# Expert outputs written in block order by ScalarE's DMA queue and gathered per token tile, sixteen blocks led by the first eight tiles

## The chip, the cores and the metric

The kernel runs on one core of one Trainium2 chip. The metric is the device time of one execution in microseconds (us), the median of several. The engines are TensorE (PE in the profile, its weight loads PEld), VectorE (DVE), ScalarE (ACT), GpSimd (POOL) and SyncE (SP, which here only issues DMAs). Each has its own instruction stream; a q behind an engine's name (ACTq) marks what its sequencer does itself: register instructions, loads of a word from SBUF into a register, branches and the issuing of DMAs.

## What is computed

Input x has 4 sequences of 512 tokens with 256 values, 2048 tokens in all. The reference, cut to what matters:

```python
x = x + attn(layernorm(x))       # linear recurrence with complex gates, two projections
xn = layernorm(x)
w, idx = gate(xn, gate_w)        # 6 of 32 experts per token, out of 4 of 8 groups
y = einsum('tei,te,edi->td', silu(xn @ w11) * (xn @ w33), c, w22)   # c: weights of the chosen experts
x = x + y + silu(xn @ sw1.T) * (xn @ sw3.T) @ sw2.T                 # shared expert
```

All values are float32. Each expert has a hidden width of 128.

## The kernel before

**Head.** The tokens are cut into 16 tiles of 128 and into 6 chunks (`CHUNKS`: 2, 2, 4, 4, 2, 2 tiles). A list of stages, written out by hand for each engine, takes the chunks through norm, recurrence, output projection, second norm, router (`logits`, `scores`, `choose`) and `places`, which works out for each token and each of its 6 experts a row in a DRAM tensor `bucket_rows`. There each expert has a bucket of its own. GpSimd sends the rows there with one indirect DMA for each tile and choice (L427, 96 in all). A row holds 256 values and, for each of 32 experts, a pair: weight and number of the row of `choice_rows` where the expert's output for this token must go.

**Table.** VectorE then works out a table of 127 blocks of 128 rows (L927 to L955): first row in `bucket_rows`, expert, column of the expert's pair. TensorE turns it into rows (L1191 to L1193), and it ends as integers in `tabs`. Around this TensorE does the shared expert (`shared_gate_up`, L1165, eight groups of 8 matmuls of 512 columns, and `shared_down`, L1178, four groups of 16 of 256 columns), with ScalarE (`shared_silu`, L612) and VectorE (`shared_hidden`, L960, `shared_out`, L964) behind it.

**Block loop.** SyncE loads the 128 rows of a block (L359) eight blocks ahead, once all rows are scattered and `tabs` is there. TensorE's step s transposes block s (L1220), makes gate and up of block s-1 (L1228, 8 matmuls) and the down projection of block s-2 (L1235). ScalarE's step s reads the expert of block s from `tabs` (L623), copies its gate and up weights (L625), copies the transposed rows (L630, waits for L1220) and applies silu to block s-1 (L617, waits for L1228). VectorE's step s multiplies silu and up of block s-1 (L985), scales the output of block s-2 (L992) and copies the pair of block s (L980). GpSimd scatters each block's output to `choice_rows` (L441, 127 indirect DMAs). Two buffers stand behind most of these steps, eight behind the outputs. Steps 16 to 63 run in hardware loops of 16 steps on the engines, the others are written out.

**Sum.** `choice_rows` has the six outputs of a token one behind another. From step 70 on SyncE loads them by tile (L367, 768 KB each), and VectorE adds them to `resid` one by one (L1016), at most two per step. ScalarE issues twelve stores (L646). The last tiles come after the last block; TensorE sums one of them (L1261).

## Time and profile before

| | us |
|---|---|
| median of 3 runs (lowest, highest) | 449.61 (448.42, 450.6) |
| the profiled execution | 450.83 |
| its span | 449.1 |

| part of the span | from | to |
|---|---|---|
| head, to the first transposes of a block | 0 | 228.4 |
| block loop, to the last scaled output | 228.4 | 432.2 |
| rest: last scatters, loads, sums, stores | 432.2 | 449.1 |

The profile has the busy time of each engine, the span in 40 slices, the chain of work that ended last, groups of instructions, and a timeline with start and length of each instruction. In the timeline a bracket holds the idle time of the engine ahead of an instruction and what ended it; "issue" is idle time with nothing in the profile that was waited for. What a sequencer does itself stands under the engine's name with a q, and does not count as busy.

### The profile page before, as it was taken

What the parts mean: (1) busy time and instruction counts of PE and PEld (TensorE: products, weight loads), DVE (VectorE), ACT (ScalarE), POOL (GpSimd) and SP (SyncE); (2) the same over time, 40 slices, a digit from 0 to 9 for tenths busy, and PEclk for the clock granted to TensorE, in tenths of its full rate; (3) what the DMA queues carried; (4) which work ended last, traced back from release to release, by engine and by line L of the source; (5) the groups of instructions that cost most, each with busy time, mean ns of one, the idle gap of its engine ahead of it and who ended that gap; (6) DMA issues with size and microseconds to landing.
All of it is one profiled execution on the core that took longest, in us unless ns stands there. A gap on an engine that the chain in (4) does not pass through costs nothing.

```text
span 449.1 us, 9145 instructions
## 1 busy us (share of the span) xinstructions
PE 376.1 (84%) x2120; PEld 301.2 (67%) x2121; DVE 294.3 (66%) x990; ACT 260.7 (58%) x585; POOL 231.6 (52%) x242
## 2 busy tenths in 40 slices
PE   2777696965976778399889999999999998998935
PEld 2644263745645563155579999999999997997924
DVE  3669688999988824612235555555567777777982
ACT  2678978768575132011157777767777776776710
POOL 2000000752778777777516666666656665663750
PEclk9898867595785687689999999999999999999996
DMA  8990000220335999333347666666689889879724
GB/s 241 405 339 2 0 0 1 74 102 15 118 118 201 413 430 380 130 128 128 117 145 215 188 195 182 204 188 191 191 265 354 255 248 300 303 208 336 244 83 174
DMA packets 41850, 87.70 MB, mean 195 GB/s; under 512 B 7204, under 2 KB 32295, under 8 KB 41296
## 3 DMA queue, kind: packets, MB, share of 16 engines
q1 hardware_dynamic: 28384, 54.77, 36.7%
q0 software_dynamic: 10704, 30.07, 18.6%
q10 hardware_dynamic: 2720, 2.40, 1.7%
q8 instruction: 15, 0.25, 0.3%
q14 instruction: 27, 0.22, 0.2%
HBM read 49.81 MB, written 39.71 MB: 199 GB/s over the span
## 4 chain that ended last, share of the span: by engine, by line
PE 50%; DVE 19%; ACT 9%; DMA 8%; issue 8%; POOL 3%; DVEq 1%; SPq 1%; ACTq 0%; POOLq 0%
PE PS L1228 17%; PE PS L1235 8%; PE PS L1165 7%; DMA payload_and_xn_t<-choice_rows 5%; PE PS L1220 4%; PE PS L1121 3%; POOL choice_rows L441 3%; PE PS L1178 3%; DMA resid<-in_x 2%; PE PS L1076 2%; ACT L605 1%; DVE st L682 1%; PE PS L1261 1%; ACT payload_and_xn_t L555 1%; DMA choice_rows<-block_out_s,block_meta 1%
## 5 line engine op out<-in xcount | busy, mean ns | idle before, releaser
L441 POOL DMA_INDIRECT choice_rows<-block_out_s,block_meta x127 | 127.0, 1000 | 86.0 <-issue 58.3
L427 POOL DMA_INDIRECT bucket_rows<-payload_and_xn_t,dest x96 | 101.9, 1062 | 116.2 <-DVE dest L874 88.2
L1228 PE MATMUL PS<-block_rows_t,block_gate_up_weights 128*128 128x128 f32 x1016 | 134.9, 276 | 0.0
L1228 PEld LDWEIGHTS PS<-block_rows_t,block_gate_up_weights 128*128 128x128 f32 x1016 | 123.4, 192 | 1.1 <-ACT block_rows_t L630 0.9
L625 ACT ACTIVATE block_gate_up_weights<-expert_weights 128x512 f32 x127 | 80.0, 630 | 35.6 <-issue 29.6
L1235 PE MATMUL PS<-expert_weights,block_hidden_t 128*128 x254 | 76.3, 382 | 3.8 <-DVE block_hidden_t L985 3.8
L992 DVE TENSOR_SCALAR block_out_s<-PS,block_meta 128x256 f32<-128x256 f32 x127 | 61.2, 482 | 0.0
L985 DVE TENSOR_TENSOR block_hidden_t<-block_silu_t,PS 128x128 f32<-128x128 f32 x127 | 36.3, 286 | 24.2 <-ACT block_silu_t L617 22.0
L630 ACT ACTIVATE block_rows_t<-PS 128x256 f32<-128x256 f32 x127 | 46.5, 366 | 7.6 <-PE PS L1220 7.6
L1220 PE MATMUL PS<-ident,block_rows_s 128*128 128x128 f32 x254 | 48.6, 273 | 1.4 <-DVE resid L964 1.3
L980 DVE COPY block_meta<-block_rows_s 128x2 f32 x127 | 22.0, 173 | 41.7 <-issue 41.4
L617 ACT ACTIVATE block_silu_t<-PS 128x128 f32<-128x128 f32 x127 | 35.0, 276 | 18.7 <-PE PS L1228 18.0
L1220 PEld LDWEIGHTS PS<-ident,block_rows_s 128*128 128x128 f32 x254 | 35.6, 141 | 14.5 <-DVE resid L964 1.7
L1016 DVE TENSOR_TENSOR resid<-resid,payload_and_xn_t 128x256 f32<-128x256 f32 x90 | 37.8, 421 | 10.1 <-DMA payload_and_xn_t<-choice_rows 9.2
L1235 PEld LDWEIGHTS PS<-expert_weights,block_hidden_t 128*128 128x128 f32 x254 | 38.5, 192 | 4.9 <-issue 4.9
L1165 PE MATMUL PS<-payload_and_xn_t,sw_s 128*128 128x512 f32 x64 | 33.3, 676 | 1.2 <-DVE turn_abs L960 1.2
L1121 PE MATMUL PS<-w_in_and_w_out,block_rows_s 128*128 128x256 f32 x96 | 25.8, 418 | 0.4 <-DVE block_rows_s L797 0.4
L1165 PEld LDWEIGHTS PS<-payload_and_xn_t,sw_s 128*128 128x128 f32 x64 | 13.8, 219 | 17.8 <-issue 16.0
L1076 PE MATMUL PS<-expert_weights,gate_blockdiag 128*128 128x256 f32 (+1 forms) x48 | 22.6, 634 | 1.7 <-ACT expert_weights L499 1.5
L1121 PEld LDWEIGHTS PS<-w_in_and_w_out,block_rows_s 128*128 128x128 f32 x96 | 20.3, 213 | 4.6 <-issue 0.7
L605 ACT ACT_TABLE_LOAD x18 | 23.1, 1283 | 0.3
L1087 PE MATMUL PS<-ident,payload_and_xn_t 128*128 128x128 f32 x32 | 7.4, 392 | 15.9 <-ACT payload_and_xn_t L555 12.0
(185 smaller groups left out, 459.1 us busy)
## 6 DMA issues: line engine op xcount, KB each, us to landing
block_rows_s<-bucket_rows SPq DMA_DIRECT2D x127, 160.0 KB
payload_and_xn_t<-choice_rows SPq DMA_DIRECT2D x16, 768.0 KB, 6.5
bucket_rows<-pad_rows SPq DMA_DIRECT2D x1, 5120.0 KB, 26.3
expert_weights<-in_experts SPq DMA_DIRECT2D x1, 4224.0 KB, 14.0
expert_weights<-in_experts SPq DMA_DIRECT2D x1, 3456.0 KB, 16.3
expert_weights<-in_experts SPq DMA_DIRECT2D x1, 2688.0 KB, 18.3
resid<-in_x SPq DMA_DIRECT2D x4, 512.0 KB, 9.3
choice_rows<-block_out_s,block_meta POOLq DMA_INDIRECT x127, 3.2
```

Source lines behind the costliest of these rows:

```text
L427: nc.gpsimd.indirect_dma_start(out=bucket_ap[:, :], out_offset=bass.IndirectOffsetOnAxis(ap=dest[:, t, k:k + 1], axis=0), in_=PAY[:, t, :] ...
L441: nc.gpsimd.indirect_dma_start(out=choice_ap[0:rows, :], out_offset=bass.IndirectOffsetOnAxis(ap=meta_id[:, slot, 1:2], axis=0), in_=yy[:, ...
L625: A(ws[:, r, :], W[:, bass.ds(first, KD * 2 * P)], ACT.Copy)
L630: A(xT[:, r, :], PS[:, r, 0:D], ACT.Copy).then_inc(s_xt, 1)
L985: TT(hh[:, r, :], sg[:, r, :], PS[:, 2 + r, P:2 * P], M).then_inc(s_hh, 1)
L992: TSC(yy[:, slot, :], PS[:, 6 + r, 0:D], meta[:, weight, 0:1], None, M).then_inc(s_y, 1)
L1016: ins = TT(resid[:, n, :], resid[:, n, :], RINGS[:, n % RING, k, :], AD)
L1121: ins = mm(PS[:, 6 + t // 2, (t % 2) * D:(t % 2 + 1) * D], PROD[h][:, t * P:(t + 1) * P], wt, start=False, stop=(n == len(parts) - 1 and t ...
L1165: ins = mm(PS[:, bank, :], sw13_s[:, k, g, h * P:(h + 1) * P], XN2T[:, b, k, :], start=(k == 0), stop=(k == KD - 1))
L1220: ins = nc.tensor.transpose(PS[:, r, k * P:(k + 1) * P], xs[:, slot, k * P:(k + 1) * P], ident[:])
L1228: ins = mm(PS[:, 2 + r, g * P:(g + 1) * P], ws[:, r, (2 * k + g) * P:(2 * k + g + 1) * P], xT[:, r, k * P:(k + 1) * P], start=(k == 0), st ...
L1235: mm(PS[:, 6 + r, 0:D], hh[:, r, :], W[:, bass.ds(w + KD * 2 * P, D)], start=True, stop=True).then_inc(s_yp, 1)
```

## The change

- **Rows** hold 256 values and 32 weights: `ROW` is 288, not 320. `choose` and the padding lose the row numbers, two VectorE instructions per chunk.
- **Outputs** go to a DRAM tensor `bucket_outputs` in which each block's 128 rows follow one another. ScalarE's queue issues one plain DMA of 128 KB per block (`write_block`), four steps after the block's first step; its row is a fourth column of `tabs`, loaded for four blocks at once. The tensor is first filled with zeros by five DMAs of SyncE's queue during the head (16.6 MB in all, `s_clear`).
- **Gathers**: GpSimd no longer scatters outputs. For each token tile it gathers six times 128 rows of `bucket_outputs` into a ring of four tiles (96 indirect DMAs of 128 KB), as soon as enough blocks are written (`blocks_through`) and the ring's place is free. VectorE makes one add per step from step 59 on (`add_choice`), 70 up to step 128, and 26 after it. SyncE issues all stores. TensorE's sum of a tile is gone.
- **Leading blocks**: the first sixteen blocks of the table are whole blocks of the first eight tiles (`early_blocks`, some twenty small VectorE instructions ahead of `choose(4)`), so their loads wait for three chunks' scatters and not for six. The table has nine phases (288 entries per quantity, before 160) and four quantities (before three).
- **Order before the loop**: on TensorE `positions(4)`, `positions(5)` stand behind the first `shared_gate_up`, and a third one stands ahead of the table's matmuls. On VectorE the first two `shared_hidden` stand ahead of the table and inside it, and `output_rows` and `output_sources` come between the later ones.
- **Loops**: bodies of 8 steps over steps 8 to 119 on TensorE and ScalarE.

```diff
-    ROW = D + 2 * E
+    ROW = D + E
-    LP = 16
+    LP = 8
-    UNROLL_AT = 64
-    RING = 6
+    LOOPED = BLOCKS // LP * LP
+    RING = 4
+    EARLY_BLOCKS = 16
+    EARLY_TILES = 8
+    FIRST_ADD = 59
+    WRITE_LAG = 4
...
+            for n in range(NCH - 1):
+                part = slice(n * BLOCKS // (NCH - 1), (n + 1) * BLOCKS // (NCH - 1))
+                sp.wait_ge(s_gp, n + 1)
+                sp.dma_start(outputs_ap[part.start * P:part.stop * P].rearrange("(j p) d -> p j d", p=P),
+                             PADT[:, 0:D].unsqueeze(1).to_broadcast([P, part.stop - part.start, D])).then_inc(s_clear, 16)
...
-                nc.gpsimd.indirect_dma_start(
-                    out=choice_ap[0:rows, :], out_offset=bass.IndirectOffsetOnAxis(ap=meta_id[:, slot, 1:2], axis=0),
-                    in_=yy[:, slot % NY, :], in_offset=None,
-                    bounds_check=last_row, oob_is_err=False).then_inc(s_ys[slot % NY], 16)
+            def gather_outputs(n):
+
+                all_written(pool, blocks_through(phase_of(n)))
+                pool.wait_ge(s_src, n // TS + 1)
+                if n < RING:
+                    pool.wait_ge(s_resid, B)
+                for k in range(TOPK):
+                    if n >= RING:
+                        pool.wait_ge(s_added, added(n - RING, k))
+                    nc.gpsimd.indirect_dma_start(
+                        out=RINGS[:, n % RING, k, :], out_offset=None, in_=outputs_ap[0:BLOCKS * P, :],
+                        in_offset=bass.IndirectOffsetOnAxis(ap=source[:, n, k:k + 1], axis=0)).then_inc(s_cin[n % RING][k], 16)
...
+            first_outputs = [act.alloc_register(f"first_output{q}") for q in range(4)]
+
+            def write_block(j, u):
+
+                if u % 4 == 0:
+                    act.reg_load(first_outputs, tabs[0:1, bass.ds(j + 3 * P, 4)])
+                act.wait_ge(s_y, j + 1)
+                row = act.snap(first_outputs[u % 4], min_val=0, max_val=2 * P * P - P)
+                act.dma_start(outputs_ap[bass.ds(row, P), :], yy[:, u % NY, :]).then_inc(s_ys[u % NY], 16)
...
-            def store(n):
-                act.wait_ge(s_fin, n + 1)
-                act.dma_start(out_d[n], resid[:, n, :]).then_inc(s_out_act, 16)
+                if not isinstance(s, int) or s >= WRITE_LAG:
+                    write_block(s - WRITE_LAG, (u - WRITE_LAG) % LP)
...
-            with act.Fori(LP, UNROLL_AT, LP) as i:
+            with act.Fori(LP, LOOPED, LP) as i:
...
+            c.add(TT(PICKS, quant[:], PER_V.unsqueeze(1).to_broadcast([P, 4, V5]), M))
+            c.wait()
+            c.add(V.tensor_reduce(tabf[:, 0:4], PICKS, X, AD))
...
+            for m in range(done, NT * TOPK):
+                add_choice(*divmod(m, TOPK))
```

The first place is ScalarE's loop body. Before, a step is these seven rows; L623 is the word of `tabs`, L617 silu:

```order
L617 ACTIVATE block_silu_t<-PS 128x128 [waits block_gate_up_psum]
L623 ISA
L623 TENSOR_LOAD tabs
L624 ISA
L625 ACTIVATE block_gate_up_weights<-expert_weights 128x512
L629 REGISTER_ALU
L630 ACTIVATE block_rows_t<-PS 128x256 [waits block_transposed_psum]
```

In the changed kernel the same stretch, silu to the copy of the weights, reads so in a step that also loads four rows of the table:

```order
L643 ACTIVATE block_rows_t<-PS 128x256 [waits block_transposed_psum]
L630 ACTIVATE block_silu_t<-PS 128x128 [waits block_gate_up_psum]
L650 ISA
L650 TENSOR_LOAD tabs
L651 REGISTER_ALU
L652 ISA [waits block_out]
L653 DMA bucket_outputs<-block_out_s 128x256
L636 ISA
L636 TENSOR_LOAD tabs
L637 ISA
L638 ACTIVATE block_gate_up_weights<-expert_weights 128x512
```

Between silu of one block and the weights of the next there now stand the register instructions and the DMA of the write, and in every fourth step a second load.

The second place is TensorE between the head's stages and the table. Before:

```order
L1165 MATMUL PS<-payload_and_xn_t,sw_s 128x512 [waits gates,shared_weights_loaded]
...
L1165 MATMUL PS<-payload_and_xn_t,sw_s 128x512 [waits ln2_transposed]
...
L1133 MATMUL PS<-member,tri 128x32 [waits bucket_rows_known,projected,membership]
...
L1191 MATMUL PS<-ident,tabf 1x128 [waits block_table_columns,bucket_rows_known]
L1192 MATMUL PS<-ident,tabf 1x128
L1193 MATMUL PS<-ident,tabf 1x128
L1165 MATMUL PS<-payload_and_xn_t,sw_s 128x512 [waits shared_hidden]
```

And now (L1275 is the old L1165, L1242 the old L1133, L1303 the table):

```order
L1275 MATMUL PS<-payload_and_xn_t,sw_s 128x512 [waits gates,shared_weights_loaded]
...
L1242 MATMUL PS<-member,tri 128x32 [waits bucket_rows_known,projected,membership]
...
L1275 MATMUL PS<-payload_and_xn_t,sw_s 128x512 [waits ln2_transposed]
...
L1275 MATMUL PS<-payload_and_xn_t,sw_s 128x512 [waits shared_hidden]
...
L1303 MATMUL PS<-ident,tabf 1x128 [waits block_table_columns,bucket_rows_known]
```

The positions moved ahead of the second group of shared matmuls, and a third group moved ahead of the table.

## Rows read from the trace of the kernel before

**Rows 1.** The page: granted clock (tenths) and data in 40 slices; one group.

```profile
PEclk9898867595785687689999999999999999999996
...
GB/s 241 405 339 2 0 0 1 74 102 15 118 118 201 413 430 380 130 128 128 117 145 215 188 195 182 204 188 191 191 265 354 255 248 300 303 208 336 244 83 174
...
L1016 DVE TENSOR_TENSOR resid<-resid,payload_and_xn_t 128x256 f32<-128x256 f32 x90 | 37.8, 421 | 10.1 <-DMA payload_and_xn_t<-choice_rows 9.2
```

**Rows 2.** Timeline in the hardware loop: start, us, engine, line, operation, [idle before].

```profile
290.71 0.97 PEld L1228 LDWEIGHTS PS<-block_rows_t,block_gate_up_weights 128*128 128x128 f32 x8
...
291.09 0.63 ACT L625 ACTIVATE block_gate_up_weights<-expert_weights 128x512 f32 x1 [0.45 <-issue]
...
291.62 0.36 ACT L630 ACTIVATE block_rows_t<-PS 128x256 f32<-128x256 f32 x1
...
291.91 0.28 ACT L617 ACTIVATE block_silu_t<-PS 128x128 f32<-128x128 f32 x1
...
292.63 0.63 ACT L625 ACTIVATE block_gate_up_weights<-expert_weights 128x512 f32 x1 [0.44 <-issue]
...
293.80 0.97 PEld L1228 LDWEIGHTS PS<-block_rows_t,block_gate_up_weights 128*128 128x128 f32 x8
```

**Rows 3.** Timeline of a written-out step in which ScalarE issues a store.

```profile
341.61 0.28 ACT L617 ACTIVATE block_silu_t<-PS 128x128 f32<-128x128 f32 x1 [0.24 <-PE PS L1228]
341.61 0.36 ACTq L646 DMA_DIRECT2D out<-resid  x1
...
341.95 0.97 PEld L1228 LDWEIGHTS PS<-block_rows_t,block_gate_up_weights 128*128 128x128 f32 x8
...
342.74 0.63 ACT L625 ACTIVATE block_gate_up_weights<-expert_weights 128x512 f32 x1 [0.86 <-issue]
...
343.69 0.97 PEld L1228 LDWEIGHTS PS<-block_rows_t,block_gate_up_weights 128*128 128x128 f32 x8 [0.17 <-ACT block_rows_t L630]
```

**Rows 4.** Sequencer work by line, ns min/median/max: L623 at 276-301 and 340-345, L359.

```profile
L623 ACTq TENSOR_LOAD <-tabs x16: 274/492/525, 276.9 to 299.7; - x16
...
L623 ACTq TENSOR_LOAD <-tabs x4: 275/284/613, 340.1 to 344.9; - x4
...
L359 SPq FUSED_REGOPS  x127: 42/42/48, 224.1 to 417.9; - x127
...
L359 SPq DMA_DIRECT2D block_rows_s<-bucket_rows x127: 337/338/445, 224.3 to 418.1; - x127
```

**Rows 5.** Timeline from the table to the first block.

```profile
177.75 0.20 PE L1135 MATMUL PS<-member,ones 128*128 128x32 bf16 x2
...
180.39 0.32 DVE L927 SCALAR_TENSOR_TENSOR block_rows_s<-bucket_next 128x160 int32<-128x160 f32 x1
...
184.28 0.65 DVE L948 TENSOR_REDUCE tabf<-block_rows_s 128x3 f32<-128x480 f32 x1
...
188.12 6.31 PE L1165 MATMUL PS<-payload_and_xn_t,sw_s 128*128 128x512 f32 x8 [1.23 <-DVE turn_abs L960]
...
197.72 7.03 PE L1165 MATMUL PS<-payload_and_xn_t,sw_s 128*128 128x512 f32 x16
...
220.72 0.96 POOL L427 DMA_INDIRECT bucket_rows<-payload_and_xn_t,dest  x1 [0.30 <-issue]
...
227.13 1.22 DVE L964 TENSOR_TENSOR resid<-resid,PS 128x1024 f32<-128x1024 f32 x1 [3.81 <-PE PS L1178]
...
228.40 0.95 PE L1220 MATMUL PS<-ident,block_rows_s 128*128 128x128 f32 x4 [1.31 <-DVE resid L964]
```

**Rows 6.** Busy time by stretch: length; PE, PEld, DVE, ACT, POOL; clock, DMA share, GB/s.

```profile
350.00:375.00 25.00, 23.51 (x182) 21.72 (x181) 17.77 (x61) 17.12 (x46) 14.64 (x15) 1.00 0.83 256
```

**Rows 7.** Timeline of the end: last scaled block output, last store issued.

```profile
431.70 0.48 DVE L992 TENSOR_SCALAR block_out_s<-PS,block_meta 128x256 f32<-128x256 f32 x1
...
446.93 0.34 ACTq L668 DMA_DIRECT2D out<-block_rows_s  x1
```

**Rows 8.** The chain that ended last: start, length, what.

```profile
433.77 2.07 DMA choice_rows<-block_out_s,block_meta
```

More of the change, by code:

```diff
@@ L349, in _, with rows_scattered, load_block @@
             sp.wait_ge(s_outp, NCH)
-            for i in range(NCH):
-                sp.wait_ge(s_scat[i], 16 * TOPK * CHUNKS[i][2])
-            def load_block(j, slot, taken):
+            def rows_scattered(first, end):
+                for i in range(first, end):
+                    sp.wait_ge(s_scat[i], 16 * TOPK * CHUNKS[i][2])
+            early_chunks = next(i + 1 for i in range(NCH) if CHUNKS[i][0] * TS + CHUNKS[i][1] + CHUNKS[i][2] == EARLY_TILES)
+            rows_scattered(0, early_chunks)
+            first_rows = [sp.alloc_register(f"first_row{q}") for q in range(4)]
+            def load_block(j, u, taken):
+                if u % 4 == 0:
+                    sp.reg_load(first_rows, tabs[0:1, bass.ds(j, 4)])
                 if taken is not None:
@@ new lines, in _ @@
+            for j in range(EARLY_BLOCKS):
+                load_block(j, j, j - NXS + 1 if j >= NXS else None)
+            rows_scattered(early_chunks, NCH)
+            with sp.Fori(EARLY_BLOCKS, FIRST_STORE, LP) as i:
+                for u in range(LP):
+                    load_block(i + u, u, i + (u - NXS + 1))
+            with sp.Fori(0, STORE_TURNS, 1) as turn:
+                for u in range(TURN_ADDS):
+                    j = turn * TURN_ADDS + (FIRST_STORE + u)
+                    load_block(j, u, j - (NXS - 1))
+                    if u % (2 * TOPK) < 2:
+                        store_tile(u // (2 * TOPK) * 2 + u % (2 * TOPK), turn)
@@ L962, in shared_out, with output_sources @@
+            def output_sources(g):
+                at_least(dve, s_src, g)
+                dve.wait_ge(s_added, 1)
+                for t in range(TS):
+                    c.add(V.max(dv[:, t, :], dpos[:, g * TS + t, :]))
+                c.wait()
+                TSC(source[:, g * TS:(g + 1) * TS, :], dv[:, :, 0:TOPK], -1.0, None, AD).then_inc(s_src, 1)
             def shared_out(b):
@@ L974, in _ @@
                     shared_hidden(b + 1, 1)
+                if b == 0:
+                    output_rows()
+                if b > 0 and b + 1 < B:
+                    output_sources(b - 1)
+            for g in range(B - 2, B):
+                output_sources(g)
             def take_meta(j, slot, loads):
                 dve.wait_ge(s_xs[slot % NXS], loads)
-                col = dve.value_load(tabs[0:1, bass.ds(j + 2 * P, 1)], min_val=D, max_val=D + 2 * (E - 1))
-                V.tensor_copy(meta[:, slot, :], xs[:, slot % NXS, bass.ds(col, 2)]).then_inc(s_meta, 1)
+                col = dve.value_load(tabs[0:1, bass.ds(j + 2 * P, 1)], min_val=D, max_val=D + E - 1)
+                V.tensor_copy(meta[:, slot, :], xs[:, slot % NXS, bass.ds(col, 1)]).then_inc(s_meta, 1)
             def hidden(j, r):
@@ L1024, in _ @@
+            for s in range(LP + 3):
                 step(s, s)
-            with dve.Fori(LP, UNROLL_AT, LP) as i:
+            with dve.Fori(LP + 3, FIRST_ADD, LP) as i:
                 for u in range(LP):
-                    step(i + u, u)
-            for s in range(UNROLL_AT, BLOCKS + 2):
-                step(s, s)
-                for n in range(NT):
-                    if n in ADD_AT and ADD_AT[n] <= s < ADD_AT[n] + TOPK // ADD_RATE[n]:
-                        for _ in range(ADD_RATE[n]):
-                            add_choice(*divmod(adds["done"], TOPK))
@@ L1034, in _ @@
-            while adds["done"] < PE_SUM * TOPK:
-                add_choice(*divmod(adds["done"], TOPK))
-            for k in range(TOPK):
-                add_choice(NT - 1, k)
+                    step(i + u, u + 3)
+            with dve.Fori(0, ADD_TURNS, 1) as turn:
+                for u in range(TURN_ADDS):
+                    step(turn * TURN_ADDS + (FIRST_ADD + u), FIRST_ADD + u)
+                    add_choice(*divmod(u, TOPK), turn)
+            done = ADD_TURNS * TURN_ADDS
+            for s in range(FIRST_ADD + done, BLOCKS + 2):
+                step(s, s)
+                add_choice(*divmod(done, TOPK))
+                done += 1
```

415 lines of the change are left out of this document (226 added, 189 removed).

## The prediction

> **What bounds the kernel now.** I read the page first. TensorE's granted clock is at the higher of its two levels (2.4 GHz) nearly from the middle of the span to the end, where the block loop lies [rows 1]. Next the timeline of the loop. The weight loads of block s (L1228) begin at 290.71 and those two blocks later at 293.80, so a step takes 1.545 us [rows 2], and 127 steps make 196 of the 203.8 us between the first transposes at 228.40 [rows 5] and the last scaled output, 431.70 + 0.48 = 432.18 [rows 7]. TensorE sets this pace, but ScalarE is not far behind: in one step it starts the copy of the weights at 291.09, the copy of the transposed rows at 291.62, silu at 291.91, and the next weights at 292.63 [rows 2], with no idle time but "issue", its own sequencer. Last I read both ends: what frees the first block at 228.4 [rows 5], and what comes behind 432.2 [rows 7, 8].
>
> **The writes on ScalarE's queue.** This is the largest term. ScalarE and TensorE hold each other in a circle two blocks long, since weights and transposed rows have two buffers. From the start of the weight loads of block k to silu of block k: 291.91 - 290.71 = 1.20. From silu to the next weights: call it X, here 292.63 - 291.91 = 0.72. From there to the end of the copy of the rows: 291.62 - 291.09 + 0.36 = 0.89 [rows 2], and some 0.06 until TensorE starts block k+2. The circle is 2.15 + X and has two steps of time, 3.09; TensorE waits when X is above 0.94. The trace has one case to test this on. At 341.61 ScalarE issues a store of 0.36 right behind silu; X becomes 342.74 - 341.61 = 1.13, and TensorE starts block k+2 at 343.69 where 341.95 + 1.545 = 343.50 was due, 0.19 late, as 1.13 - 0.94 says [rows 3].
>
> In the changed kernel every step has such a DMA between silu and weights. A DMA with a row from a register takes 0.338 on its sequencer, a register instruction around 0.04 [rows 4], and a write has two or three: 0.44 in all. To what does that add? X in a looped step was 0.72 with a word's load of about 0.5, and such a load takes from 0.27 to 0.51 in the loop [rows 4]. So X is 0.72 + 0.44 = 1.16 with slow loads and 1.16 - 0.22 = 0.94 with fast ones. I take 1.06, between them, because in the written-out part the loads are mostly fast (0.284 of 0.275 to 0.613) and in the loop mostly slow (0.492) [rows 4], and the changed kernel's SyncE loads only every fourth step, so there is less to collide with. Every fourth step has a second load, of four words, with an instruction of 0.05 ahead. The trace has no load of four words; by the loads of one it is 0.33 to 0.66, and I take 0.45, the middle. These loads always hit the same of the two interleaved circles (the body has 8 steps, an even number), and the slower one sets the pace. Over four steps it needs 2 x (2.15 + X) + 0.45 = 6.87, or 1.717 per step, 0.172 over 1.545. ScalarE's loop has 112 steps (8 to 119): **+19.3 us**. With X at 0.94 and 0.33 it is 6.51 / 4 = 1.627, +9.2. With X at 1.16, another 0.107 if the issue takes 0.445 as SyncE's longest does [rows 4], and 0.66, it is 7.49 / 4 = 1.873, +36.8. The twelve written-out steps with a write have X near 0.8 to 0.9 and exceed the circle only with the four-word load: +0.6. Below nothing this term can't go: TensorE's own work is the 1.545.
>
> What a page says on this stands apart from the sum. The Trainium skill, Perfetto Trace Analysis, section on the hardware DMA instruction, says that the reported time of such an instruction includes waiting for a lock on the descriptor generator that two sequencers share. SyncE's range of 0.337 to 0.445 agrees with it weakly [rows 4]; if every write waited for a whole issue of SyncE, X would grow by 0.34 and the loop by a further 19 us.
>
> **What leaves the loop.** Of 25 us from 350 to 375 TensorE idles 1.5 [rows 6], and the stretch from 400 to 426 reads alike. In these VectorE waits for tiles of 768 KB that arrive late, with TensorE behind it. The gathers come earlier: tiles 0 and 1 can be gathered from about step 52, twelve of them take GpSimd some 15 us at the 0.96 + 0.30 per indirect DMA of the scatters [rows 5], and the first add is at step 59. Each later pair is likewise some ten steps ahead. **-3.0 us**. VectorE's step has one add of 0.421 [rows 1] where it had up to two, but more waits on registers; it keeps some 0.2 to 0.3 of slack at 1.717 per step, and I cost it at nothing.
>
> **The head.** Before, two things ended almost together: the shared expert, with `shared_out` at 227.13 + 1.22, and the scatters, the last of them issued at 220.72 for 0.96 [rows 5], with the first load of a block 2.6 behind it, at 224.3 [rows 4]. The leading blocks take the second out. The first moves little. TensorE has 10.3 us between 177.8, when the first positions are being made behind the second group of shared matmuls, and the third group at 188.12 [rows 5], of which positions and table fill 1.8. It now puts the third group in there. But VectorE's table, 180.39 to 184.93 before [rows 5], grows: 288 entries for 160, and the product and the reduction over four quantities have 1152 elements where 480 took 0.65 [rows 5], so about 1.4 each. With the two longer scans, three more products and a shared product of 0.7 inside, the table takes some 11.5. Places come some 3 us sooner, so it begins at 178 and ends near 189.5; with 1.3 for the matmuls TensorE goes on at 191. What is left then (five groups of 3.5, as 7.03 for two shows, four `shared_down` of about the same, some 1.4 of waiting for the last silu and product, and 2.8 for one group at the lower clock, as 6.31 for 3.5 shows [rows 5]) is 35.7, and the end 226.7, against 227.1. Each `choose` lacks 0.5 of VectorE's work, some of it on the path: 1 us more. Together **-1.5 us**, from +2 to -8.5. The zeros cost nothing: five writes of 3.3 MB from 20 us on, and from the fourth slice to the eleventh (34 to 123 us) the page has 0 to 118 GB/s where others have 400 [rows 1]. `output_rows` and `output_sources` lie beside TensorE's shared matmuls.
>
> **The end.** From 432.18, where the last output is scaled, to 449.1 is 16.9 us before [rows 7]. Now GpSimd is late. Tiles 12 and 13 need 115 blocks; the last of these is written by ScalarE at step 118, ten steps ahead of the last scaled output (which I call 0), and lands some 2.1 later [rows 8]. So their twelve gathers begin at -13.4 and take 12 x 1.26 to 1.7. Tile 14 follows to 9.3 and tile 15 to 16.8. The last gather lands 2.2 on, at 18.7; the last add takes 0.43, and the store 449.1 - 446.93 = 2.2 [rows 7]: 21.4. VectorE's 26 adds (11 us) hide behind the gathers. **+4.5 us**, from 0 if a gather takes 1.0, to +8.
>
> **Sum.** -1.5 - 3.0 + 19.3 + 0.6 + 4.5 = +19.9. The span becomes 469.0, and with the 1.7 us around it 470.7, against the profiled 450.8, which is itself 1.2 above the median. I give 470.
>
> **Rivals.** *ScalarE hides the writes.* For it: a sequencer runs ahead of its engine when it needn't wait; and the Trainium skill, DMA: Bandwidth & Descriptors, section on issuing engines, calls the sequencer's time for starting a DMA usually small beside the DMA. Against it: the 0.19 at 343.69, after just one such issue [rows 3]. Then all is as above without 19.9 of the loop: 450.8.
>
> *The head gives more, and the writes are hidden too; faster.* The point is when the table ends: if VectorE has it by 184, TensorE has no gap at all in the shared expert, and 10.3 - 1.8 = 8.5 come off and not 1.5. 450.8 - 8.5 - 3.0 + 4.5 = 443.8. VectorE would have to do the larger table in 6 us, and X would have to stay under 0.94; against that stand the 0.65 for 480 elements and the 0.36 of an issue [rows 3, 5].
>
> *The loop is slower still.* VectorE with its waits on registers becomes the bound, or the writes wait for the lock, or TensorE's clock falls to its lower level in the new gaps. At 1.9 per step it is +40 in the loop: 492. The gaps of 0.2 in each step are short, and in 350 to 375 the clock stayed at 1.00 with 1.5 us of idle time [rows 6].
>
> **Numbers.** Forecast, loop bound by ScalarE, 455 to 489: 0.75. Writes hidden, about 451: 0.09. Faster: 0.07. Slower still: 0.09. From 451 to 489 holds about 0.8. A measurement can tell about 0.5% from no change. Faster by over 0.5% (under 447.4): 0.08; within: 0.07; slower: 0.85.
>
> **What would show it.** In the profile after, looped steps are 1.63 to 1.87 long, TensorE's weight loads of L1228's successor wait for ScalarE's copy of the transposed rows in most of them, and silu to weights is 0.94 to 1.3, with a DMA of 0.34 inside. Steps longer by 0.3 come every fourth. The first transposes come at 225 to 228, and behind the last scaled output lie some 21 us, with gathers back to back. Wrong I'd be if X stayed under 0.94, if the wait before those weight loads named VectorE or a block's load, or if gathers began late enough to hold up adds in the loop.

## The result: 476.1 us, slower by 5.8%

| | before | after |
|---|---|---|
| median, us (lowest, highest, of 4 runs each) | 450.11 (448.42, 450.67) | 476.09 (474.18, 477.0) |
| span of the profiled execution | 449.1 | 475.2 |
| head, to the first transposes | 228.4 | 226.8 |
| block loop, to the last scaled output | 203.8 | 221.8 |
| rest | 16.9 | 26.6 |

The ratio is 1.058, with a 95% interval from 1.053 to 1.062. The difference of the spans is -1.6 + 18.0 + 9.7 = 26.1 us.

**The loop.** First the page of the changed kernel, its group for the weight loads of gate and up: engine, operation and count, then busy time and mean of one, then idle time ahead and what ended it.

```profile
L1339 PEld LDWEIGHTS PS<-block_rows_t,block_gate_up_weights 128*128 128x128 f32 x1016 | 123.9, 192 | 16.5 <-ACT block_rows_t L643 13.5
```

In the kernel before the same group had 1.1 us of idle time:

```profile
L1228 PEld LDWEIGHTS PS<-block_rows_t,block_gate_up_weights 128*128 128x128 f32 x1016 | 123.4, 192 | 1.1 <-ACT block_rows_t L630 0.9
```

Now TensorE waits for ScalarE's copy of the transposed rows (L643): in 89 of the 127 blocks its weight loads begin within 0.06 us of the end of that copy, before in 7. Two looped steps of ScalarE in the timeline, against [rows 2]:

```profile
331.98 0.28 ACT L630 ACTIVATE block_silu_t<-PS 128x128 f32<-128x128 f32 x1
332.12 0.34 ACTq L653 DMA_DIRECT2D bucket_outputs<-block_out_s  x1
...
332.98 0.63 ACT L638 ACTIVATE block_gate_up_weights<-expert_weights 128x512 f32 x1 [0.73 <-issue]
...
333.52 0.36 ACT L643 ACTIVATE block_rows_t<-PS 128x256 f32<-128x256 f32 x1
...
333.66 0.36 ACTq L653 DMA_DIRECT2D bucket_outputs<-block_out_s  x1
...
333.78 0.27 ACT L630 ACTIVATE block_silu_t<-PS 128x128 f32<-128x128 f32 x1
333.94 0.97 PEld L1339 LDWEIGHTS PS<-block_rows_t,block_gate_up_weights 128*128 128x128 f32 x8
...
334.77 0.63 ACT L638 ACTIVATE block_gate_up_weights<-expert_weights 128x512 f32 x1 [0.72 <-issue]
```

From weights to weights this step takes 334.77 - 332.98 = 1.79 us. Silu starts 0.80 behind the weights copy, as soon as the copy of the rows lets it; it waits for nobody. TensorE begins at 333.94, right behind the end of that copy at 333.88. Then the sequencer works off the write and the load of a word, and the next weights wait 0.72 us for "issue". So ScalarE is the bound of this step. The profile puts 19.5 us of ScalarE's idle time ahead of weights copies down to VectorE's outputs, which the writes wait for. That is no real wait: from step 8 to step 124 each output was finished at least 1.8 us before its write was issued. What one item costs its sequencer stands in the rows of the lines (least, median, longest, in ns):

```profile
L653 ACTq DMA_DIRECT2D bucket_outputs<-block_out_s x127: 337/343/384, 233.6 to 448.8; - x127
```

```profile
L650 ACTq TENSOR_LOAD <-tabs x32: 310/316/502, 233.1 to 447.1; - x32
```

```profile
L636 ACTq TENSOR_LOAD <-tabs x127: 278/287/720, 220.6 to 444.0; - x127
```

**One long stall.** In the stretch of [rows 6] TensorE is now busy for 21.85 us, at a mean granted clock of 0.94; in the stretches before and behind it, 24.50 and 24.53 at 1.00:

```profile
350.00:375.00 25.00, 21.85 (x149) 19.07 (x148) 14.98 (x49) 14.03 (x38) 14.62 (x16) 0.94 0.78 231
```

```profile
371.78 0.29 DVE L1094 TENSOR_TENSOR block_hidden_t<-block_silu_t,PS 128x128 f32<-128x128 f32 x1 [3.46 <-issue]
...
372.21 1.22 PE L1346 MATMUL PS<-expert_weights,block_hidden_t 128*128 x2 [2.65 <-DVE block_hidden_t L1094]
...
373.44 1.83 PEld L1339 LDWEIGHTS PS<-block_rows_t,block_gate_up_weights 128*128 128x128 f32 x8
```

VectorE's hidden product comes 3.46 us late with nothing waited for. It is the first instruction of the second turn of VectorE's 24-step loop (steps 59 to 106; this is step 83). TensorE waits 2.65 us. Behind this idle time the granted clock is at the lower of its two levels (0.52 from 373.4 to 375.3 us), and eight weight loads take 1.83 us and not 0.97. The two steps last 5.04 and 2.40 us. The loop's own rows show where the stall begins:

```profile
L1136 DVEq COMPARE_BRANCH  x2: 55/59/63, 368.0 to 413.0; - x2
```

```profile
L1133 DVEq COMPARE_BRANCH  x6: 50/56/72, 258.7 to 326.7; - x6
```

The branch at 368.0 is the jump back of the 24-step body, and VectorE's next instruction begins 3.73 us behind it. Behind the branch at 413.0, which ends that loop, it takes 0.45 us, and behind the six branches of the 8-step loop 0.45 to 0.59.

**The end.** The last output is scaled by 448.62. The timeline from there, last rows:

```profile
448.14 0.48 DVE L1101 TENSOR_SCALAR block_out_s<-PS,block_meta 128x256 f32<-128x256 f32 x1 [0.22 <-PE PS L1346]
```

```profile
465.14 0.95 POOL L461 DMA_INDIRECT payload_and_xn_t<-bucket_outputs,output_rows  x1 [0.30 <-issue]
...
467.90 0.42 DVE L1129 TENSOR_TENSOR resid<-resid,payload_and_xn_t 128x256 f32<-128x256 f32 x1 [0.78 <-DMA payload_and_xn_t<-bucket_outputs,output_rows]
468.35 0.33 SPq L385 DMA_DIRECT2D out<-resid  x1
```

SyncE is through with its last store at 470.2. But the span ends at 475.2. What fills the rest are the closing instructions of the engines, here those of GpSimd and SyncE (duration in ns, start in us):

```profile
L78 POOLq DRAIN  x1: 19700/19700/19700, 455.3 to 455.3; - x1
...
L78 SPq DRAIN  x1: 7/7/7, 470.2 to 470.2; - x1
```

GpSimd's drain ends at 455.3 + 19.7 = 475.0, that is 8.9 us behind the end of the last gather's issue (466.09). In the kernel before it ended at 436.7, 2.0 us behind the issue of the last scatter (433.77 to 434.75), under work that ran on to 449.

### The profile page after: what moved, and what is told of

Same layout as the page of the kernel before. It is cut to its first block, busy times and chain, and to the rows that moved or that the text cites. A ratio compares the mean times of both kernels' runs of the same rounds, so it can differ in the third digit from the quotient of the medians.

```text
span 475.2 us, 9648 instructions
## 1 busy us (share of the span) xinstructions
PE 386.5 (81%) x2113; PEld 302.4 (64%) x2114; DVE 309.8 (65%) x1050; ACT 253.5 (53%) x584; POOL 195.5 (41%) x209
## 4 chain that ended last, share of the span: by engine, by line
PE 30%; ACTq 18%; issue 16%; DVE 15%; ACT 14%; DMA 3%; DVEq 1%; POOL 1%; SPq 0%
ACTq L653 8%; ACTq L636 7%; PE PS L1339 6%; PE PS L1275 5%; PE PS L1288 3%; PE PS L1230 3%; ACT block_rows_t L643 2%; PE PS L1222 2%; DMA resid<-in_x 2%; PE PS L1220 2%; ACTq L650 2%; ACT block_gate_up_weights L638 2%; DVE resid L1129 2%; PE PS L1185 2%; DVE st L693 2%
## 5 line engine op out<-in xcount | busy, mean ns | idle before, releaser
L461 POOL DMA_INDIRECT payload_and_xn_t<-bucket_outputs,output_rows x96 | 92.6, 964 | 153.5 <-issue 114.4
L445 POOL DMA_INDIRECT bucket_rows<-payload_and_xn_t,dest x96 | 100.4, 1046 | 116.3 <-DVE dest L882 87.9
L1339 PE MATMUL PS<-block_rows_t,block_gate_up_weights 128*128 128x128 f32 x1016 | 142.4, 283 | 5.0 <-ACT block_rows_t L643 3.8
L1339 PEld LDWEIGHTS PS<-block_rows_t,block_gate_up_weights 128*128 128x128 f32 x1016 | 123.9, 192 | 16.5 <-ACT block_rows_t L643 13.5
L643 ACT ACTIVATE block_rows_t<-PS 128x256 f32<-128x256 f32 x127 | 46.5, 366 | 7.7 <-PE PS L1331 7.7
L1089 DVE COPY block_meta<-block_rows_s 128x1 f32 x127 | 19.6, 154 | 45.6 <-issue 45.1
L1129 DVE TENSOR_TENSOR resid<-resid,payload_and_xn_t 128x256 f32 (+1 forms) x96 | 40.9, 426 | 9.7 <-DMA payload_and_xn_t<-bucket_outputs,output_rows 6.1
L1275 PE MATMUL PS<-payload_and_xn_t,sw_s 128*128 128x512 f32 x64 | 32.7, 668 | 0.0
L1275 PEld LDWEIGHTS PS<-payload_and_xn_t,sw_s 128*128 128x128 f32 x64 | 13.6, 215 | 15.8 <-issue 15.7
L1185 PE MATMUL PS<-expert_weights,gate_blockdiag 128*128 128x256 f32 (+1 forms) x48 | 21.6, 610 | 1.7 <-ACT expert_weights L512 1.5
```

The costliest lines, as they stand in the source:

```text
L445: nc.gpsimd.indirect_dma_start(out=bucket_ap[:, :], out_offset=bass.IndirectOffsetOnAxis(ap=dest[:, t, k:k + 1], axis=0), in_=PAY[:, t, :] ...
L461: nc.gpsimd.indirect_dma_start(out=RINGS[:, n % RING, k, :], out_offset=None, in_=outputs_ap[0:BLOCKS * P, :], in_offset=bass.IndirectOffs ...
L643: A(xT[:, r, :], PS[:, r, 0:D], ACT.Copy).then_inc(s_xt, 1)
L1129: TT(total, total, RINGS[:, slot, k, :], AD).then_inc(s_added, 1)
L1275: ins = mm(PS[:, bank, :], sw13_s[:, k, g, h * P:(h + 1) * P], XN2T[:, b, k, :], start=(k == 0), stop=(k == KD - 1))
L1339: ins = mm(PS[:, 2 + r, g * P:(g + 1) * P], ws[:, r, (2 * k + g) * P:(2 * k + g + 1) * P], xT[:, r, k * P:(k + 1) * P], start=(k == 0), st ...
```

## The experiments

All ran beside the kernel before. The kernel before had medians from 447.0 to 450.7 in the different sets of runs, so the ratios are the better comparison.

| kernel | median, us | ratio to before (95%) | loop, us | rest, us |
|---|---|---|---|---|
| changed kernel | 476.09 | 1.058 (1.053, 1.062) | 221.8 | 26.6 |
| e1_sp | 460.86 | 1.023 (1.015, 1.032) | 205.5 | 28.6 |
| e2_before_silu | 461.55 | 1.024 (1.016, 1.033) | 205.9 | 27.8 |
| e3_no_turn_loop | 472.21 | 1.049 (1.041, 1.058) | 219.6 | 26.3 |
| e4_pool_waits | 477.92 | 1.063 (1.054, 1.071) | 222.7 | 27.8 |
| e5_drains (one run) | 470.57 | | 221.8 | 21.4 |
| e6_load_more | 475.42 | 1.063 (1.058, 1.069) | 222.5 | 26.1 |
| e7_both | 455.75 | 1.020 (1.014, 1.025) | 200.8 | 27.5 |
| e8_cut | 452.58 | 1.010 (1.006, 1.014) | 201.4 | 23.9 |
| e9_load_each | 491.97 | 1.093 (1.086, 1.099) | 239.0 | 25.5 |
| e10_drains_hidden | 450.27 | 1.002 (1.000, 1.005) | 200.5 | 22.1 |
| e11_one_drain | 447.49 | 0.999 (0.995, 1.002) | 200.5 | 20.1 |
| e12_before_drain (one run) | 452.9 | | 205.7 | 16.1 |

**e1_sp: the writes on SyncE's queue.**

```diff
@@ sync
+            def write_block(j, u):
+                if u % 4 == 0:
+                    sp.reg_load(first_outputs, tabs[0:1, bass.ds(j + 3 * P, 4)])
+                sp.wait_ge(s_y, j + 1)
...
@@ scalar
-                if not isinstance(s, int) or s >= WRITE_LAG:
-                    write_block(s - WRITE_LAG, (u - WRITE_LAG) % LP)
```

> One part of the change undone alone: SyncE's queue issues the writes of finished blocks (10 steps behind, as in the kernel before, with its register loads), everything else is the changed kernel's. Theory (ScalarE's sequencer sets the looped step): the gate and up period falls from its mean of 1.70 us to 1.545 us, so the block loop is 0.155 x 112 = 17.4 us shorter, and the time comes to 476.1 - 17.4 = about 458.7 us; ScalarE's wait that TensorE shows for block_rows_t (13.5 us in all) goes. Rival (something else of the change slows the loop, for instance GpSimd's gathers or the sixteen leading blocks' transfers): the period stays near 1.70 us and the time at 476 us. The end, 26.6 us behind the last scaled output, stays in both.

The loop is 16.3 us shorter, the period back at 1.56 us but for the stall at step 83, and the ratio falls by 0.035, some 15.6 us. So the writes on ScalarE's queue are the larger part of the loss in the loop. This run also writes ten steps behind the block's first and not four, and its rest is 2.0 us longer; the next one keeps the four steps.

**e2_before_silu: the writes on ScalarE, ahead of silu.**

```diff
+                if not isinstance(s, int) or s >= WRITE_LAG:
+                    write_block(s - WRITE_LAG, (u - WRITE_LAG) % LP)
                 if not isinstance(s, int) or 1 <= s <= BLOCKS:
                     silu(s - 1, (u - 1) % 2)
-                if not isinstance(s, int) or s >= WRITE_LAG:
-                    write_block(s - WRITE_LAG, (u - WRITE_LAG) % LP)
```

> The writes stay on ScalarE, but stand between ScalarE's copy of the rows and its silu in every step, and no longer between the silu and the next copy of the weights. Theory (what counts is the stretch X from the end of silu to the start of the next weights copy, which must be under 0.94 us in a period of 1.545 us): the sequencer works the write off while the copies still run, X falls under 0.94 us, and the time comes to about 459 us, at most 463 us. Rival A (ScalarE's total work of a step is too long wherever the write stands): 476 us. Rival B (the write holds back the silu, and the silu the down product): a period over 1.70 us and over 480 us.

The same instructions on the same engine, ahead of silu and not behind it, cost next to nothing in the loop: it is 205.9 us, 15.9 less and level with e1, and a step takes 1.556 us over the steps 17 to 80. A step in its timeline:

```profile
301.44 0.63 ACT L638 ACTIVATE block_gate_up_weights<-expert_weights 128x512 f32 x1 [0.23 <-issue]
301.75 0.34 ACTq L653 DMA_DIRECT2D bucket_outputs<-block_out_s  x1
301.97 0.36 ACT L643 ACTIVATE block_rows_t<-PS 128x256 f32<-128x256 f32 x1
302.24 0.27 ACT L630 ACTIVATE block_silu_t<-PS 128x128 f32<-128x128 f32 x1
302.64 0.63 ACT L638 ACTIVATE block_gate_up_weights<-expert_weights 128x512 f32 x1
```

The DMA is issued while the engine still copies the weights. What counts is not how much the sequencer does in a step, but how much of it stands where the engine has nothing queued. Rivals A and B fall.

**e3_no_turn_loop: VectorE's turns written out.**

```diff
-            with dve.Fori(0, ADD_TURNS, 1) as turn:
-                for u in range(TURN_ADDS):
-                    step(turn * TURN_ADDS + (FIRST_ADD + u), FIRST_ADD + u)
-                    add_choice(*divmod(u, TOPK), turn)
-            done = ADD_TURNS * TURN_ADDS
+            done = 0
```

> VectorE's two turns of 24 steps with the additions are written out instead of looped; no work is added or taken away. Theory (the stall of 3.46 us at 371.78 us, ahead of a hidden product with nothing waited for, is the jump back at the end of the first turn, and the lower clock behind it is its echo): both go, 5.04 + 2.40 - 2 x 1.70 = 4.0 us, so 472.1 us. Rival (the stall belongs to something at that time, a transfer or a count, not to the jump): it stays, 476 us.

The median is 3.9 us lower. The profiled loop is 2.2 us shorter; the head, which is the same code, differs by another 2.4 us between the two executions. In its profile the stall is gone, VectorE's "issue" ahead of the hidden product falls from 3.9 to 0.8 us, and the clock stays at 1.00:

```profile
350.00:375.00 25.00, 24.06 (x176) 21.28 (x174) 17.25 (x59) 15.52 (x44) 14.66 (x16) 1.00 0.88 253
```

So the stall belongs to the jump back of the long body. It came at the same step in all seven executions that kept this loop (the changed kernel, e1, e2, e4, e5, e6 and e9), 3.1 to 3.8 us long, at times from 360 to 381 us, so it is not something that happens at one time. Shorter bodies don't have it: 0.45 to 0.59 us behind the branches of the 8-step loop here, 0.39 to 0.64 us behind those of the 16-step loop of the kernel before. What the engine waits for, the DMA queues of the changed kernel suggest, in the window from 368.0 to 371.8 us (packets, MB, share of the engines):

```profile
q14 instruction: 2, 0.02, 1.7%
```

Two packets on the queue that carries instructions lie in the stall. The Trainium skill, Runtime: NRT & Kernel Launch, section on instruction fetch mechanics, says that a taken branch to a place that is no longer held makes the engine wait for a fetch. The packets and the length of the body agree with it. They don't show it: single packets on this queue also come in stretches without a stall, in e3 one from 368.0 to 371.8 us, and the trace doesn't say which engine a packet was for.

**e4_pool_waits: GpSimd waits for the last addition before its drain.**

```diff
             for n in range(NT):
                 gather_outputs(n)
+            pool.wait_ge(s_added, added(NT - 1))
```

> GpSimd waits, behind its last gather, for VectorE's last addition, and only then comes to its closing drain. Nothing else is changed. Theory A (the drain runs for as long as the descriptors of the last gathers need to be worked off, about 8.9 us from the last gather's issue, whatever GpSimd does meanwhile): the wait passes at about 468.3 us and the end stays at 475.2 us, 476 us. Theory B (the drain's long time comes from its meeting the gathers while they are in flight): behind the wait it takes about 2 us, GpSimd is done by 470.5 us, and the time falls by 4 to 5 us to about 471.5 us. A drain that costs its full length from the wait on would end at 477 us or later.

Neither theory: the last of the expected cases came out. The drain starts at 465.4, when every gather has landed and been added, and still takes its full length.

```profile
L78 POOLq DRAIN  x1: 8885/8885/8885, 465.4 to 465.4; - x1
```

So it isn't waiting for data: here the 8.9 us count from its own start, and not from the last gather.

**e5_drains: drains behind the scatters and behind 48 gathers.**

```diff
+            nc.gpsimd.drain()
             for n in range(NT):
+                if n == NT // 2:
+                    nc.gpsimd.drain()
                 gather_outputs(n)
```

> The changed kernel with two more drains on GpSimd: one behind its 96 scatters (where it then stands idle for about 100 us) and one behind the first 48 gathers; 48 gathers and the closing drain follow. In the last experiment the closing drain took 8.885 us although GpSimd had been idle and every gather had landed; in the kernel before it was done 2.0 us after the last scatter. Theory A (the length goes with the number of gathers since the last drain): the one behind the scatters is short (2 us or less), the other two about 4.5 us each, and the end comes about 4.4 us nearer to the last gather. Theory B (it goes with all indirect transfers since the last drain, 192 in the changed kernel): each of the three is about 4.5 us (96, 48 and 48: 4.4, 2.2, 2.2). Theory C (a fixed price of a drain that finds the queue empty): each is 8.9 us. The block loop's time is not the question here.

```profile
L465 POOLq DRAIN  x1: 23065/23065/23065, 204.1 to 204.1; - x1
```

```profile
L468 POOLq DRAIN  x1: 14369/14369/14369, 375.5 to 375.5; - x1
```

```profile
L78 POOLq DRAIN  x1: 14024/14024/14024, 454.3 to 454.3; - x1
```

**e6_load_more: one more load, that nothing reads.**

```diff
+                act.reg_load(spare, tabs[0:1, bass.ds(j + P, 1)])
                 act.reg_load(expert, tabs[0:1, bass.ds(j + P, 1)])
```

> The changed kernel with one more one-word register load on ScalarE, ahead of the one that each weights copy needs, into a register that nothing reads: X (end of silu to the next weights copy) grows by about 0.33 us (a load of 0.287 and its address of 0.05) in every step. Theory (circle of two blocks, a step is half of 2.15 + X where that is over 1.545 us): the looped step grows by 0.165 us where X is already over its threshold and less elsewhere, 112 x 0.15 to 0.165 = +17 to +18.5 us, so about 493 to 495 us. Rival (a step pays for the whole of a sequencer's item): +0.33 x 112 = +37 us, 513 us. Rival (the sequencer has room): 476 us.

This tells nothing about the theories. Only the old line's 127 loads are in the trace; the compiler left the dead one out, so this is the changed kernel once more.

```profile
L638 ACTq TENSOR_LOAD <-tabs x127: 273/288/944, 217.5 to 441.6; - x127
```

It serves as a repeat: 475.42 us. Its head ends at 223.7 and not at 226.8, which shows how far heads differ from one execution to the next.

**e9_load_each: the dose, with loads that are used.**

```diff
-                if u % 4 == 0:
-                    act.reg_load(first_outputs, tabs[0:1, bass.ds(j + 3 * P, 4)])
+                act.reg_load(first_outputs, tabs[0:1, bass.ds(j + (3 * P - u % 4), 4)])
```

> The changed kernel with the load of four words on ScalarE in every step and not in every fourth: 84 more loads of about 0.31 us (and 0.05 for the address) in the looped steps, each of them used. In the run before this one the added load had been left out by the compiler, so that it was the changed kernel over again. Now the steps with such a load have X (start of silu to start of the next weights copy) at 1.2 to 1.3 us, the others at 0.72 to 1.01 us; with it in all, X is about 1.2 us everywhere. Theory P (the prediction's circle of two blocks: a step is half of 2.15 + X): 1.68 us per step at X = 1.2, as now, so 474 to 480 us; with the prediction's own X of 1.51 for such a step 1.83 us, +14.6, 491 us. Theory S (ScalarE's own order is the circle: weights copy to silu takes 0.80 us, then X, so a step is 0.80 + X): 2.00 us per step, +0.30 x 112 = +34 us, about 510 us.

492 us is the number of theory P with the prediction's X, but the trace has another reason for it. Two steps of ScalarE:

```profile
320.31 0.27 ACT L630 ACTIVATE block_silu_t<-PS 128x128 f32<-128x128 f32 x1
320.43 0.34 ACTq L652 DMA_DIRECT2D bucket_outputs<-block_out_s  x1
321.29 0.63 ACT L638 ACTIVATE block_gate_up_weights<-expert_weights 128x512 f32 x1 [0.70 <-issue]
321.82 0.36 ACT L643 ACTIVATE block_rows_t<-PS 128x256 f32<-128x256 f32 x1
322.09 0.27 ACT L630 ACTIVATE block_silu_t<-PS 128x128 f32<-128x128 f32 x1
```

Over the steps 17 to 80, with A from the start of the weights copy to the start of silu, and X from there to the next weights:

| kernel | A, us | X, us | step, us | steps with A up to 0.81 | (2.15 + X) / 2, slower circle |
|---|---|---|---|---|---|
| before | 0.93 | 0.62 | 1.547 | 9 of 64 | 1.41 |
| changed | 0.82 | 0.89 | 1.709 | 55 of 64 | 1.60 |
| e9_load_each | 0.80 | 1.04 | 1.846 | 64 of 64 | 1.65 |

The last column takes X over every second step, since the prediction has two interleaved circles and lets the slower one set the pace: 0.67, 1.04 and 1.15.

A step is A + X by definition; what tells the theories apart is that A stands at its floor of 0.80, where silu follows the copies and has not waited for TensorE. Theory S has the circle right: ScalarE's own order, a step of 0.80 + X, TensorE idle behind it, here in the page of e9:

```profile
L1338 PEld LDWEIGHTS PS<-block_rows_t,block_gate_up_weights 128*128 128x128 f32 x1016 | 123.8, 192 | 33.6 <-ACT block_rows_t L643 30.9
```

That is 33.6 us where the changed kernel had 16.5. Theory P's circle, with the X that was measured, is 0.11 us short of the changed kernel's step and 0.19 short of e9's. What S had wrong was X: it rose by 0.15 and not by 0.3. On average the write's DMA was issued 0.03 us ahead of silu's start in the changed kernel and 0.11 behind it in e9. So only some 0.14 us of the added loads fell behind silu's start, and the rest fell where ScalarE still had its copies to do.

**e7_both: e2 and e3 together; e8_cut: e7 with tile 12 as a phase of its own.**

```diff
-    CUTS = [[2], [2], [2, 4], [2, 4], [2], [1, 2]]
+    CUTS = [[2], [2], [2, 4], [2, 4], [1, 2], [1, 2]]
```

> The write ahead of the silu and VectorE's turns written out, together. If the two causes are separate, their gains add up: 476.1 - 14.6 - 3.9 = about 457.6 us, which is still 7.5 us above the kernel before; the whole of that is then the end (27.8 us behind the last scaled block against 16.9). If the stall at the turn's end only hid behind the slower loop, it stays near 461 us.

> The last one, with one more phase: tile 12 gets a phase of its own (cuts after one and two tiles in the chunk of tiles 12 and 13), so that its gathers may go when 109 of 127 blocks are written, and need not wait for 115. Now 24 gathers run back to back from 420.2 us to 450.6 us, as GpSimd stands idle before that; with six of them ahead of that wait, 18 follow, 7.5 us less, limited by the last tile, whose six gathers can go only about 5 us after the last scaled block (5 + 6 x 1.25 = 12.5 against 18.7 us): so -6 us, to about 451 to 452 us, less 0.3 to 0.6 us given back in the head for a tenth phase of 32 columns. Rival (the additions on VectorE, one in a step, keep the ring of four tiles full and the gathers late): no more than -1.5 us, 456 us.

e7 gives 1.020: within the noise the two gains add up (0.033 of e2 and 0.008 of e3; together 0.038). Its loop of 200.8 us is 3.0 shorter than that of the kernel before, and TensorE has no gap in the stretch of [rows 6]:

```profile
350.00:375.00 25.00, 25.00 (x192) 23.02 (x192) 18.61 (x64) 17.94 (x47) 13.64 (x16) 1.00 0.91 273
```

In e8 the last gather is issued 14.8 us behind the last scaled output (18.4 in e7), and the rest falls by 3.6 us. That is less than the 6 expected, because GpSimd is now busy without a gap from 396.5 us on.

**e10_drains_hidden, e11_one_drain: e8 with drains where GpSimd stands idle.**

```diff
+            nc.gpsimd.drain()
             for n in range(NT):
+                if n in (6, 8, 10):
+                    nc.gpsimd.drain()
                 gather_outputs(n)
```

In e11 the condition is `n == 6`.

> The last version (write ahead of silu, VectorE's turns written out, a phase of its own for tile 12), with drains on GpSimd at the places where it stands idle anyway: behind the scatters and ahead of the gathers of tiles 6, 8 and 10 (idle 4.0, 4.3 and 4.4 us). Theory A (a drain's length goes with the gathers since the last one): about 3 us ahead of tile 6 (36 gathers), 1 to 1.5 us ahead of tiles 8 and 10 (12 each), and some 3 us at the end (36) instead of 8.9. The end is then set by the last gather's landing, addition and store, about 4.5 us behind the last gather's issue, so 4.4 us less: 448.2 us. Rival (a fixed price of a drain, 4 us or more whenever gathers ran): the drains ahead of tiles 8 and 10 take 4 us and the last one 4 us, which gives 449 to 453 us.

> As the last version, without its drains ahead of tiles 8 and 10. There the drains took 3.6 and 4.0 us from the end of the last gather's issue (12 gathers each) and GpSimd needed another 1.1 us until its next gather, so the gathers of tile 10 began at 398.8 us and not at 396.5 us, and the last gather was issued by 444.2 us and not by 442.3 us. Without them the last gather should be issued by about 442.3 to 442.9 us. The closing drain then has 60 gathers behind it and not 36: it took 3.3 us with 36, 3.9 us with 48 and 8.9 us with 192, so 4 to 5 us with 60, which ends at 447 us, where the last store ends too (about 4.1 us behind the last gather's issue). Span 447.0 us, 448.7 us in the median, 1.5 us below the last version and level with the kernel before (within 0.5%). If the closing drain went by the time in the loop or by all 192, it would be 8.9 us again, and the time 452 us.

The closing drain took 3.3 us with 36 gathers behind it (e10) and 5.0 with 60 (e11). The one ahead of tile 6, with 36 gathers behind it as well, took 4.5 in e10 and 5.1 in e11. In e10 those ahead of tiles 8 and 10, with 12 gathers each, took 3.6 and 4.0, not the 1 to 1.5 of theory A, and the next gather came another 1.1 later, so they made the gathers late; e11 leaves them out. With the last gather issued at 440.1 and the drain's end at 445.1, e11 is the best version, and level with the kernel before: 0.999 (0.995 to 1.002). No version was measurably faster than the kernel before.

**e12_before_drain: a drain behind the row scatters of the kernel before.**

```diff
             for i in range(NCH):
                 scatter_rows(i)
+            nc.gpsimd.drain()
```

> The kernel before with one drain on GpSimd behind its 96 scatters of rows, ahead of the 127 scatters of finished blocks. Its closing drain, with 223 scatters behind it, was done 2.0 us after the last one. If a drain's length goes with the number of indirect transfers since the last drain, whatever they are, the first takes about 8 us here (as the drain at the same place in the changed kernel, 7.9 us) and the last becomes shorter than 2.0 us. If the scatters of finished blocks are cheap to drain for a reason of their own, the last one stays at 2.0 us. The time is 450 us in either case, since GpSimd has room there (the first block is scaled about 35 us after the last row scatter).

```profile
L433 POOLq DRAIN  x1: 23098/23098/23098, 208.8 to 208.8; - x1
```

```profile
L69 POOLq DRAIN  x1: 4022/4022/4022, 435.6 to 435.6; - x1
```

7.9 us behind the 96 scatters of rows, again, and 2.0 behind the 127 of blocks, as without the extra drain. So a drain's length is not simply a count. At the end it took 3.3 us for 36 gathers, 4.0 for 48, 5.0 for 60 and 8.9 for 96 gathers with 96 scatters ahead; in the middle of the loop 12 gathers already took 3.6 and 4.0, and 36 took 4.5 and 5.1. What sets the length, and why 127 scatters of blocks need only 2.0, stays open.

## Why the prediction was right, and where it was right by luck

| term | predicted | measured |
|---|---|---|
| head | -1.5 | -1.6 here; -1.6 to -4.7 over nine executions with the same head |
| stalls that leave the loop | -3.0 | -3.0 (e7's loop against before) |
| writes on ScalarE | +19.3 + 0.6 | +15.9 (e2) and +16.3 (e1); +18.8 (e3's loop against e7's) |
| VectorE's turn | none | +5.1 (e2's loop against e7's); +2.2 (the changed kernel's against e3's) |
| end | +4.5 | +9.7 |
| sum | +19.9 | +26.1 |

The sum came out within the range in part by luck. The writes were put 1 to 4 us too high, and 2.2 to 5.1 us of the turn and 4.8 us of the drain had no term. What the writes and the turn cost depends on which is taken out first; together they are 21.0 us (the changed kernel's loop against e7's).

**The head** went as said, within what executions differ by. VectorE's table ended at 189.8 and TensorE went on with the shared matmuls at 190.9, where 189.5 and 191 were predicted. The first block's load came at 192.4, far from the path.

**The stalls** of the late tiles went, and nothing took their place in VectorE's steps but the turn.

**The writes: the size was met, the mechanism was not.** The step that failed is the circle of two blocks, (2.15 + X) / 2 with its threshold of 0.94. It was tested on [rows 3], a single late issue. There the step before it had left slack: silu had waited for TensorE (0.24 in its bracket) and could close up to 0.80 behind the weights afterwards. When every step has the write, that slack is used up once, and ScalarE's own chain is the bound: 0.80 + X, threshold 1.545 - 0.80 = 0.745. The term X failed as well: 1.06, and 1.17 with the four-word load spread over four steps, where 0.89 was measured; in the slower circle alone 1.29 predicted and 1.04 measured. The loads took 0.287 and 0.316 and not 0.45, and the sequencer issues part of its items ahead of silu's start. Too weak a circle and too long an X cancel: 1.717 predicted, 1.709 found. The prediction would call itself wrong if X stayed under 0.94. The mean of 0.89 did, though single steps went up to 1.40, so the reasoning was wrong here, and only the forecast stood.

**The lock.** The prediction gave waiting for a shared descriptor generator another 19 us as an aside, after the Trainium skill, Perfetto Trace Analysis. In the changed kernel the issues on ScalarE's sequencer took 337 to 384 ns and SyncE's block loads 332 to 353, so no such wait shows there. Elsewhere the medians are 333 to 355, with a rare longer one: a block load of 972 ns in e2, a write of 471 in e7 and one of 728 in e11. What those waited for is not shown.

**VectorE's turn** had no term. VectorE was costed at nothing, by its instructions; the jump at the end of a long body was not looked at.

**The end.** The chain of gathers was right: last gather issued 17.5 us behind the last scaled output (16.8 predicted), SyncE through 21.6 behind it (21.4; its own terms, 16.8 + 2.2 + 0.43 + 2.2, give 21.6). What failed is that the end was taken to be the last store. GpSimd's closing drain lasts 4.8 us longer.

**The rivals.** "ScalarE hides the writes" did not come about as the code stands, but e2 shows it can, with two lines exchanged. The Trainium skill, DMA: Bandwidth & Descriptors, section on issuing engines, calls the sequencer's time for starting a DMA usually small beside the DMA. By that alone its cost can't be told here: the writes, with 0.34 us of issue each, cost 0.16 per step in one place and 0.01 in another (1.709 and 1.556 against 1.547).

## What to carry over

- Test a recurrence on a stretch where it recurs. A single late instruction shows how much slack there is, and not what happens when every step draws on it; for each engine in the circle, also add up its own order alone.
- In an engine's stream, put what only the sequencer does (DMA issues, register loads) behind an instruction that the engine will still be busy with, and not where it has run dry.
- An engine that has long been off the path can still end the kernel: read the closing instructions of each engine, not only its last work.

## What was new about the hardware

- GpSimd's drain behind indirect DMAs is work of its own: 8.9 us at the end of the changed kernel, also when all gathers had landed and been added (e4). A drain placed earlier shortens the last one (4.0 with 48 gathers in e5, 3.3 with 36 in e10), but a drain behind 12 gathers still took 3.6 and 4.0, and one behind 127 scatters 2.0.
- A jump back over a loop body of 24 steps stopped VectorE for 3.1 to 3.8 us in seven executions, and in the changed kernel TensorE's granted clock was at its lower level behind it (0.52). Without the loop both were gone. Bodies of 8 and 16 steps had 0.39 to 0.64 us behind their branches.
- A load of four words into registers takes hardly longer (median 0.316 us) than that of one (0.287) in the changed kernel.
